# A graph network of four layers on one core: planning reordered, sums of squares moved from pass five to pass six, and the last normalisation cut into four chunks

## The reference

```python
x = _layernorm(x + L0(x))   # 3 times: t = x @ W.T + b; x = (t + segment_sum(t[src], dst)) / 2, relu between
x = _layernorm(x + L1(x))   # GCN with degree norm
x = _layernorm(x + L2(x))   # GCN with degree norm and PReLU
x = _layernorm(x + L3(x))
# L3, the part that matters here:
hihj = concat([x[src], x[dst]])
exp_e = exp(silu(bn(hihj @ Wf + bf)));  we = weight[src] * exp_e
a = we / segment_sum(we, dst)[dst]
z = silu(bn(einsum('ed,hdk->ehk', hihj, Wg) + bg))
h = segment_sum(a * z, dst)
out = bn(h, n_gamma, n_beta) + x         # bn over all nodes, then the last layer norm over features
```

## Time and profile before

| | us |
|---|---|
| median of 3 runs | 6757.25 (6753.95 to 6762.34) |
| the profiled execution, its own time | 6749.94 |
| its span, first to last instruction | 6748.3 |
| busy: PE / DVE / ACT / POOL | 4055.1 / 3483.0 / 2599.6 / 1716.9 |

### The profile page before, as it was taken

One profiled execution on the slowest core, in us unless ns is written; L12 is line 12 of the kernel. 1 busy time (PEld: TensorE's weight loads), 2 busy tenths in 40 slices (PEclk: granted clock), 3 DMA queues, 4 the chain that ended last, 5 costly groups with the idle time before them and its releaser, 6 DMA issues.

```text
span 6748.3 us, 117320 instructions
## 1 busy us (share of the span) xinstructions
PE 4055.1 (60%) x30833; PEld 3494.4 (52%) x30834; DVE 3483.0 (52%) x11972; ACT 2599.6 (39%) x5401; POOL 1716.9 (25%) x2055
## 2 busy tenths in 40 slices
PE   5666557999999999311111111111187988888882
PEld 2222225999999999211111111111187888777772
DVE  7999886555677766100000000000027888888787
ACT  2467886444555544100000000000045666655552
POOL 1000000000000012676777677776700000000000
PEclk8887778999999999655555555555599999999996
DMA  2112224777777777533333333333384444444341
GB/s 62 59 78 90 95 97 162 256 255 260 254 260 253 259 258 254 157 108 99 110 110 108 106 112 102 108 111 107 102 273 126 132 125 123 119 113 110 106 109 51
DMA packets 316571, 975.56 MB, mean 145 GB/s; under 512 B 56932, under 2 KB 135708, under 8 KB 297548
## 3 DMA queue, kind: packets, MB, share of 16 engines
q1 hardware_dynamic: 246579, 755.43, 33.8%
q0 software_dynamic: 68320, 218.57, 11.1%
q10 hardware_dynamic: 1593, 0.80, 0.0%
HBM read 777.04 MB, written 197.54 MB: 144 GB/s over the span
## 4 chain that ended last, share of the span: by engine, by line
issue 36%; DVE 28%; PE 26%; ACT 3%; DMA 3%; DVEq 2%; ACTq 1%; SPq 0%; POOL 0%; PEld 0%; POOLq 0%; PEldq 0%
PE banks L836 21%; DVE F L1035 6%; DVE F L1036 4%; DVE E L1233 3%; DMA AB<-counts_d 2%; DVE E L1229 2%; DVE E L1240 2%; PE banks L805 1%; DVE E L1210 1%; DVE od L1127 1%; PE banks L913 1%; DVE E L1235 1%; ACT E L719 1%; PE banks L908 1%; PE banks L920 1%
## 5 line engine op out<-in xcount | busy, mean ns | idle before, releaser
L666 ACT ACTIVATE BX<-AB 128x1664 fp32r<-128x1664 uint16 x588 | 855.2, 1483 | 2385.7 <-remote 1482.0
L571 POOL DMA_INDIRECT E<-table_d,IX x1563 | 1479.9, 947 | 644.7 <-issue 644.7
L836 PE MATMUL banks<-HS,AB 128*128 128x256 f32 (+1 forms) x7350 | 1061.2, 292 | 938.4 <-issue 922.6
L836 PE MATMUL banks<-HS,BX 128*128 128x256 f32 (+1 forms) x7056 | 1045.3, 291 | 933.9 <-issue 930.8
L836 PEld LDWEIGHTS banks<-HS,AB 128*128 128x128 f32 x7350 | 974.6, 196 | 974.8 <-issue 959.3
L836 PEld LDWEIGHTS banks<-HS,BX 128*128 128x128 f32 x7056 | 954.0, 196 | 976.7 <-issue 976.6
L1075 DVE TENSOR_REDUCE US<-banks 128x128 f32<-128x256 f32 (+1 forms) x294 | 124.9, 425 | 2421.5 <-remote 1490.3
L805 PE MATMUL banks<-F 128*128 128x392 bf16 x2368 | 622.3, 413 | 399.1 <-DVE F L1036 258.7
L1035 DVE TENSOR_SCALAR F<-F,front 128x392 bf16<-128x392 f16 x2368 | 747.3, 316 | 78.1 <-PE banks L805 70.9
L548 POOL CAST HS<-TOP 128x128 f32 (+3 forms) x245 | 102.6, 419 | 2507.6 <-DVE TOP L1052 2504.4
L805 PEld LDWEIGHTS banks<-F 128*128 128x128 bf16 x2368 | 270.0, 114 | 751.4 <-issue 706.7
(11 more groups left out here) (219 smaller groups left out, 3896.7 us busy)
## 6 DMA issues: line engine op xcount, KB each, us to landing
AB<-counts_d SPq DMA_DIRECT2D x294, 832.0 KB
AB<-counts_d SPq DMA_DIRECT2D x294, 768.0 KB
E<-rows_d SPq DMA_DIRECT2D x452, 260.0 KB, 3.2
rows_d<-E POOLq DMA_DIRECT2D x99, 1040.0 KB
counts_d<-stage SPq DMA_DIRECT2D x49, 1600.0 KB, 5.2
E<-dst_d SPq DMA_DIRECT2D x452, 128.0 KB, 3.2
E<-table_d,IX POOLq DMA_INDIRECT x1563
table_d<-TR POOLq DMA_DIRECT2D x49, 65.0 KB, 3.4
```

Source lines behind the costliest of these rows:

```text
L571: g.indirect_dma_start(GS[:, t % (GSET * GSETS), :], None, table_d, bass.IndirectOffsetOnAxis(ap=IX[:, t:t + 1], axis=0)).then_inc(g_in[k] ...
L666: act.activation(BX[:, par, lo:hi], ab_low[:, par, lo:hi], ACT.Copy).then_inc(low_expanded, 1)
L836: ins = pe.matmul(agg[par][:, 0:wide], w, HS[u][:, s, 0:wide], start=(s == 0), stop=(s == NB - 1))
```

## The change

In planning:
- `pe.sem_inc(onehot_used, RING)` is the first thing that PE does; it stood ahead of the counting loop. DVE waits for `visit_keys_made` one group of 128 visits at a time; it waited for all 19 groups.
- PE no longer turns the edge lists first. They are turned after the keys of groups 6 to 18, one edge group behind each key group, and ACT copies them (`keep_edges`); DVE did.
- The window row is laid out directly after the window starts, twice: once as PSUM addresses (`bof`) and once, every fourth visit only, as window numbers (`wof`). DVE makes `plan` from it in two instructions; there were four.
- W0 and the first biases are loaded from ACT's queue, the node weights early on SP's, and PE turns W0 and the node weights last. The banks are taken in another order (`(k + 2) % 4`), and ACT clears two of three pairs early.

In passes 5 and 6: the two instructions that add `odeg * t * t` are taken out of `partB` of pass 5, and three in `partA` of pass 6 do it from the table's two halves.

In the last normalisation: four chunks of blocks (16, 15, 12 and 6). ACT squares, PE adds up all blocks by itself in one bank (13 matmuls with `ones`, up to 512 columns), DVE meanwhile makes `2 * X + beta`; then for each chunk two wide instructions, statistics, root on ACT, and the output rows on ACT (blocks 0 to 45) or DVE (46 to 48), each chunk with its own output transfer.

```diff
+            pe.sem_inc(onehot_used, RING)
             pe.wait_ge(consts_made, 1)
...
-            pe.wait_ge(edges_cast, 1)
-            for g in range(NG):
...
+            for k in range(NVB):
+                pe.matmul(banks_f[0:1, BO0 + k * P:BO0 + (k + 1) * P], bof[:, k:k + 1], ident[:, :],
...
+            for k in range(NVB):
+                ins = pe.matmul(banks_f[0:1, EO0 + k * 32:EO0 + (k + 1) * 32], wof[:, k:k + 1], ident[:, :].rearrange("p (c k) -> p c k", k=4)[:, :, 3],
...
             pe.wait_ge(ends_made, 1)
             for k in range(NVB):
...
+                if k == NVB - NG:
+                    pe.wait_ge(edges_cast, 1)
+                    pe.wait_ge(plan_made, 1)
+                if k >= NVB - NG:
+                    turn_edges(k - (NVB - NG))
...
-            pe.sem_inc(banks_free, 1)
-            pe.sem_inc(onehot_used, RING)
...
-            v.wait_ge(visit_keys_made, NVB)
+            v.wait_ge(edges_cast, 1)
             for n in range(NV):
+                if n % P == 0:
+                    v.wait_ge(visit_keys_made, n // P + 1)
                 if n % 4 == 0:
                     v.wait_ge(onehot_used, n + 4)
...
+                    t = HS[1][:, ds(b, 1), :].rearrange("p a f -> p (a f)").bitcast(f32)
+                    link(tt(XQ, t[:, 0:EDG], t[:, EDG:PW], ALU.add))
+                    link(stt(XQ, XQ, odeg[:, ds(b, 1)], XQ, ALU.mult, ALU.mult))
+                    link(tt(acc[:, 1, :], acc[:, 1, :], XQ, ALU.add))
...
-                    link(tt(R1[:, 0:EDG], TR[:, par, 0:EDG], TR[:, par, 0:EDG], ALU.mult))
-                    link(stt(acc[:, 1, :], R1[:, 0:EDG], odeg[:, ds(b, 1)], acc[:, 1, :], ALU.mult, ALU.add))
...
+            for c, (lo, hi) in enumerate(CK):
+                act.wait_ge(centered, c + 1)
+                act.activation(Q[:, lo:hi, 0:P], FB1[:, lo:hi, :], ACT.Square).then_inc(squared, 1)
...
+                act.wait_ge(norm_made, c + 1)
+                for b in range(lo, min(hi, MID)):
+                    act.activation(T[:, b, 0:P], FB1[:, b, :], ACT.Identity, bias=NMB[:, b:b + 1], scale=RST[:, b:b + 1]).then_inc(y_ready, 1)
...
+                pe.wait_ge(squared, c + 1)
+                for b in range(lo, hi, 4):
+                    k = min(4, hi - b)
+                    ins = pe.matmul(psV[:, 0:k * P], ones[:, :], Q[:, b:b + k, 0:P], start=(b == 0), stop=(b + k == NB), skip_group_check=True)
```

More of the change, by code:

```diff
@@ L388, in build @@
         TOPJ = NB * NTP
-        SP0 = 3 * 512
+        BO0 = 2 * 512
+        EO0 = BO0 + NVB * P
+        assert EO0 % 512 == 3 * P and EO0 + NVB * 32 <= 8 * 512
         def batch(n):
@@ L493, in _ @@
                         sp.dma_start(P4[:, h], rows_d[:, ds(t + 4 * h, 4), :]).then_inc(p_in[h], 16)
+            for lo, hi in CK:
+                sp.wait_ge(y_ready, min(hi, MID))
+                if hi == NB:
+                    sp.wait_ge(y_rest, 1)
+                full = min(hi, NB - 1)
+                sp.dma_start(out[lo * P:full * P, :].rearrange("(b p) f -> p b f", p=P), T[:, lo:full, 0:P]).then_inc(out_done, 16)
             nl = (NB - 1) * P
[L496 to L497 removed]
             sp.dma_start(out[nl:N, :], T[0:LASTN, NB - 1, 0:P]).then_inc(out_done, 16)
[L499 removed]
+            sp.wait_ge(out_done, 16 * (len(CK) + 1))
         @block.gpsimd
@@ L611, in keep, with keep_edges, clear @@
                 act.activation(KUL[:, :, k * P:(k + 1) * P], ps[k % 2][:, 0:2 * P].rearrange("p (k e) -> p k e", k=2), ACT.Copy).then_inc(visit_keys_made, 1)
+            def keep_edges(g):
+                act.wait_ge(edges_turned, g + 1)
+                act.activation(DTG[:, :, g * P:(g + 1) * P], ps[2 + g % 2][:, 0:2 * P].rearrange("p (k e) -> p k e", k=2), ACT.Copy).then_inc(turned_copied, 1)
+            def clear(pair):
+                pair = (pair + 2) % 4
+                act.activation(banks[:, 2 * pair:2 * pair + 2, 0:HJ], zero[:, 0:1].unsqueeze(1).broadcast_to([P, 2, HJ]), ACT.Copy).then_inc(bank_cleared, 2)
             for k in range(NVB):
@@ L615, in _ @@
                     keep(k - 1)
+                if k > NVB - NG:
+                    keep_edges(k - 1 - (NVB - NG))
+                if k == NVB - NG:
+                    act.wait_ge(plan_made, 1)
+                    clear(0)
+                    clear(1)
             keep(NVB - 1)
-            def clear(pair):
-                act.activation(banks[:, 2 * pair:2 * pair + 2, 0:HJ], zero[:, 0:1].unsqueeze(1).broadcast_to([P, 2, HJ]), ACT.Copy).then_inc(bank_cleared, 2)
+            keep_edges(NG - 1)
+            act.wait_ge(misc_turned, 1)
+            act.activation(W0r[:, :, :], ps[2][:, 0:3 * P].rearrange("p (l d) -> p l d", l=3), ACT.Copy).then_inc(misc_copied, 1)
+            act.activation(wn[:, :], ps[3][:, 0:NB], ACT.Copy).then_inc(misc_copied, 1)
             act.sem_inc(window_copied, WBUF)
-            act.wait_ge(banks_free, 1)
-            for k in range(3):
-                clear(k)
+            act.wait_ge(visit_keys_made, NVB)
+            clear(2)
             def copy_half(b, half, e, side):
@@ L953, in _ @@
             last_messages(last, psH[0])
-            for k in range(2):
-                pe.wait_ge(nsum_ready, k + 1)
-                pe.matmul(ps[7][:, k * P:(k + 1) * P], ones[:, :], acc[:, k, 0:P], start=True, stop=True).then_inc(nsum_done, 1)
+            pe.wait_ge(nsum_ready, 1)
+            pe.matmul(ps[7][:, 0:P], ones[:, :], acc[:, 0, 0:P], start=True, stop=True).then_inc(nsum_done, 1)
+            for c, (lo, hi) in enumerate(CK):
+                pe.wait_ge(squared, c + 1)
+                for b in range(lo, hi, 4):
+                    k = min(4, hi - b)
+                    ins = pe.matmul(psV[:, 0:k * P], ones[:, :], Q[:, b:b + k, 0:P], start=(b == 0), stop=(b + k == NB), skip_group_check=True)
+            ins.then_inc(nsum_done, 1)
         @block.vector
@@ L1319, in _, with wide @@
             mean, anr = mrow[:, 0, 0:P], drow[:, 0:P]
-            def wide(row):
-                return row.unsqueeze(1).broadcast_to([P, NB, P])
+            def wide(row, n):
+                return row.unsqueeze(1).broadcast_to([P, n, P])
             link2(ts(mean, ps[7][:, 0:P], 1.0 / N, None, ALU.mult))
```

165 lines of the change are left out of this document (89 added, 76 removed).

## The result

The changed kernel takes 6707.15 us (median of 4 runs, 6705.7 to 6708.88), the kernel before 6757.61 beside it (6753.95 to 6762.34). The ratio is 0.9925, 95% interval 0.9908 to 0.9942: 50.5 us less. The forecast was 6687; the time lies in its range (6668 to 6709), near the far end, and within 4 us of what the rival "the head start is lost" gave (6710.7). The profiled execution took 6708.35 us, its span 6706.7.

The account below looks back on a forecast made before the run. Five stages in series, each with its own bound, POOL's indirect transfers the costliest. Planning 23.6 plus last normalisation 46.6 less passes 0.1 gave 70.1 us saved: median 6757.25 to 6687, range 6668 to 6709.

Parts of the forecast that it names:

- the head start is lost: Rival: DVE stands at a full ring or counting swallows planning's gain; only the last normalisation counts, 6710.7 us; chance 0.09.
- first term: Planning: first one-hot 29 us earlier, less DVE's wait for PE, a net gain of 23.6 us, ends 15 and 31.
- the full ring: Planning: DVE's 32-visit ring of one-hots fills in 12.6 us, at 53.9, before PE takes its first.
- DVE goes on there: Planning: DVE resumes at PE's fourth count, 59.4, having stood 5.5 us.
- the second 38: Planning: window row's added 32-column instructions, taken at two thirds of the first 38, 4.1 us.
- plan at 41.1, range 37 to 48: Planning: when DVE has made the plan, so that the first one-hot comes at 41.3 instead of 70.35.
- Passes: +0.1 forecast: Passes 5 and 6: 0.9 us saved and 1.0 added in the last blocks, the rest hidden; +0.1 us together.
- The three new instructions with two SBUF inputs: Pass 6: forecast not to slow POOL's gather; rival that they do, +44 us at most, 6709 at half; chance 0.05.
- Last normalisation: -46.6 forecast: Tail: sums of squares on PE, two wide DVE instructions, rows on ACT, earlier output; 46.6 us saved, ends 37 and 52.
- The rival at half clock: Last normalisation: PE stays at half clock in the sums of squares, 7.5 us later, 6694.5 us; chance 0.12.
- The gather's pace: POOL's indirect transfers, forecast near 2125 us; rivals: slower, 0.06 us more each gives 6781, chance 0.05; faster, 0.07.

Follow-up runs that it names:

- f1_after: The changed kernel itself, run on a chip where the kernel before takes 5074 to 5078 us: 5008.83 us, ratio 0.9869 to the kernel before.
- h1_held: The changed kernel with DVE's plan and ACT's first shift of keys also waiting for the last key transfer: 6713.7 us, ratio 0.9932 to the kernel before.
- h2_after: The changed kernel unaltered, run again beside h1_held on a chip where the kernel before takes about 6757 us: 6714.47 us, ratio 0.9935.
- e5_keys_late: The changed kernel with POOL's 19 key transfers held until DVE's plan is made: 5018.38 us, ratio 0.989 to the kernel before.
- e2_passes: The kernel before with only the sums of squares moved from pass 5 to pass 6: 5075.85 us, ratio 0.9992.
- e3_tail: The kernel before with only the last normalisation done in four chunks: 5029.81 us, ratio 0.9908.
- e4_x_late: The changed kernel with the loads of X held until the plan is made: 5015.52 us, ratio 0.9868 to the kernel before.
- e1_head: The kernel before with only the planning part of the change: 5053.91 us, ratio 0.9955.
- e6_tail2: The changed kernel with smaller first chunks, roots placed within ACT's rows and more last blocks on DVE: 5002.08 us, ratio 0.9859 to the kernel before.

## Why the prediction was right, and where its first term was not

**Planning: -23.6 forecast, -7.3 measured at the end of counting.** The form of the sum held: the table above is the forecast's own step, the full ring and "DVE goes on there", in eleven runs, up to the end of counting. What failed is the sentence on the window row and what hangs on it: "Bounds for the second 38: nothing, or as dear as the first", and "plan at 41.1, range 37 to 48". The second 38 instructions, taken at two thirds of the first (4.1 us), are cheaper where PE isn't held: 2.44 us for 5.50 in f1_after. Here the row was done at 38.6, but the plan started at 52.70 and PE's first count came at 73.10, not 58.3. I costed PE beside POOL's key transfers by its pace alone and only asked whether the keys are there in time. The row that spoke of it was the clock's long stretch at half speed beside POOL's indirect transfers, and I took that for a stage of its own, without asking why PE was slow in it. In the kernel before most of that stretch was hidden: PE waited for the node weights from 39.5 to 49.47 and began the window row at 51.39, and POOL's last key transfer was issued at 47.88. On the second kind of chip, where PE works at its pace beside POOL, the term measured 22.2 by the time and 25 by the end of counting.

That the key transfers are what holds PE's signals is argued, not shown. For it: in three traces DVE's plan starts 4.4 to 4.5 us after the last transfer is issued, and in h1_held 1.2 us after ACT, which waits for its landing, starts (51.80 and 52.96); a wait for it costs nothing (h1_held); the same gaps return beside the gather; and neither is there on the second kind. Against its being enough alone: in the kernel before, on the first chip, PE turned six edge groups beside the same transfers, and beside the loads of X, without a gap, and DVE answered within 0.5 us:

```profile
35.99 3.53 PE L762 MATMUL banks<-ident,F 128*128 128x128 f32 x12 [4.34 <-issue]
37.92 0.85 DVE L999 CAST DTG<-banks 128x256 uint16<-128x256 f32 x2 [0.35 <-PE banks L762]
```

In the changed kernel PE's gaps begin at 34.84, 9.7 us behind POOL's first transfer, in h2_after at 33.31. And two rivals stand. The loads of X fill the transfer engines in the same stretch (share 1.02 to 1.07 from 32 to 48 us) and end with it (0.36 from 48 to 52), so that X, or both together, fits the end of the hold as well; only the gaps in pass 6, at a share of 0.33 to 0.39, speak against it. And it may be that the engines get their instructions late and not their signals; the traces say only "issue" and "remote". The run that would tell the key transfers from the rest is the one with the keys held back until the plan (e5_keys_late) on a chip of the first kind, and neither it nor its two repeats had one.

**Passes: +0.1 forecast; nothing measured** (e2_passes, 0.9981 to 1.0003). DVE's wait before L1118 behind the gather is 2.40 us, forecast 2.7, and the edits lie in it. In pass 5 the two removed instructions only made DVE's wait for PE longer, 1.49 us in a block for 0.66. The three new instructions with two SBUF inputs leave POOL's transfer as it was, 945 ns for 947, 2129.1 us in all for 2124.6. The Trainium skill, GPSIMD Engine Reference, section Key points, has them contend; no row here shows it. It isn't ruled out either: on the first kind only some 18 of the 49 blocks of pass 6 lie beside the gather. On the second kind all do, and on one chip of it the gather took 2120.7 and 2115.2 us with the three (e2_passes, e4_x_late), 2113.5 and 2099.8 without (e3_tail, e1_head); the time of e2_passes leaves room for some 2 us at most.

**Last normalisation: -46.6 forecast; -47.3 in the trace, -46.3 alone** (e3_tail). Its steps, counted from the sum for the mean: PE's sums begin at 5.1 us (5.1 forecast), sums of squares done at 17.5 (18.9), first wide instruction at 20.4 (21.7), last row at 55.5 (56.3), end at 59.7 (60.4). PE's 49 blocks took 12.40 us, forecast 13.9. The granted clock was 0.50 to 6654, 0.83 in the next 4 us and 1.00 after that, so it came back about as in planning. Most of the 1.5 us is the price of a block at full clock. Four blocks are one matmul, which is two instructions in the trace; each loads weights, and the loads start 0.85 us apart at half clock and 0.43 at full clock:

```profile
6653.14 0.34 PEld L1001 LDWEIGHTS banks<-E,ones 128*128 128x128 f32 x1 [0.52 <-issue]
6653.99 0.34 PEld L1001 LDWEIGHTS banks<-E,ones 128*128 128x128 f32 x1 [0.52 <-issue]
...
6656.40 0.19 PEld L1001 LDWEIGHTS banks<-E,ones 128*128 128x128 f32 x1 [0.24 <-issue]
6656.83 0.19 PEld L1001 LDWEIGHTS banks<-E,ones 128*128 128x128 f32 x1 [0.24 <-issue]
```

So a block costs 0.215 us at full clock, where 0.25 was taken for 40 of them: 1.4 us. The rival at half clock didn't happen. A row on ACT takes 0.39 us (6.26 / 16; forecast 0.40; by the Trainium skill, ScalarE: Activation LUTs, section What ACT_TABLE_LOAD costs, an estimate of 0.386, and the trace agrees). What I had not seen is the second wait for a root, 3.27 us before the last chunk; it took the place of slack, and taking both away (e6_tail2) gave 1.0 us.

**Sum.** 7.3 and 47.3 make 54.6 us at the two ends. The two profiled executions differ by 41.6, the medians by 50.5 in the result and 43.3 in h2_after. The 4 to 13 us between stand in the gather, pass 6 and the edge pass (the table of marks above). Some 3 us are the matmuls that PE has left behind the gather; the rest, mostly in the edge pass, has no cause on record. Executions of the kernel before on one of these chips spread by 8 to 17 us, and there is one trace of it. So the 7.3 us are shown at the end of counting only, not in the time. On the second kind (f1_after) the ends make 17 and 46, and the time gives 65.6: nothing is missing.

**Rivals.** The lost head start was given 0.09; it is what happened, mostly, for another reason than those I named (the chain of PE and the keys were in time, the shared part of counting swallowed nothing, though gather and pass 6 did). That the time fell inside the range is in part luck: the range reached that far for the sake of this rival and of the half clock. The gather's pace did not move by more than 1%, on any chip: 2124.6 and 2129.1 us on the first, 2109.9 (f1_after) and 2120.7 (e2_passes) on the second kind.

## What to carry to other kernels

When a step is moved to an earlier time, ask not only what it waits for there but what it then runs beside, and look for a row of the same neighbours elsewhere in the trace: PE's "issue" gaps beside POOL's indirect transfers were to be seen in pass 6, and planning was priced without them. Then follow a head start to the end: 7 us at the end of counting were under 2 us at the end of pass 6. With a ring between two engines, the gain at the far end is the ring's depth in time, less how much later than before the producer goes on behind it, and not how much earlier its first item is. And a tail in series (reduce, root, scale, write) was priced well from its rows here, and cutting it into chunks with the writing on another engine gained 46 to 47 us.

## What the runs showed of the hardware

Two kinds of chip, with one program: 6757 us twice, 5074 to 5078 on four chips, and runs on one chip within 0.5% of each other. On the first kind PE, with nothing to wait for, issues one matmul about every 2.8 us beside POOL's gather (36 in 100 us of pass 6 against 830, f1_after), at a granted clock of 0.50 against 1.00. In planning DVE and ACT, which wait for PE's signals, start 4.4 to 4.5 us after the last key transfer is issued, at 52.5 to 53.0 us (ACT's wait in h1_held apart); on the second kind DVE starts at 34.7 to 35.9. POOL's gather as a whole takes the same on both (2124.6 and 2109.9 us). What differs between the chips no trace shows.
